# Last attention of a four-layer gated block: half of head 0's maximum taken while the scores are still computed, and the rows of reciprocals made by a matmul in the even units

## The reference, cut to what matters

```python
q = jnp.einsum('bnd,de->bne', ln, Wq)
kv_in = jnp.concatenate([xn, ln], axis=1)
kv = jnp.einsum('bnd,de->bne', kv_in, Wkv)
k, v = jnp.split(kv, 2, axis=-1)
q, k, v = (split_heads(q), split_heads(k), split_heads(v))
q = q * scale
sim = jnp.einsum('bhid,bhjd->bhij', q, k)
sim = jnp.where(full_mask[:, None, None, :], sim, max_neg)
attn = jax.nn.softmax(sim, axis=-1)
out = jnp.einsum('bhij,bhjd->bhid', attn, v)
out = out.transpose(0, 2, 1, 3).reshape(b, m, INNER)
out = jnp.einsum('bne,ed->bnd', out, Wout)
return layer_norm(out, g_o, b_o)
```

## Time and profile before

| | |
|---|---|
| median of 3 runs | 2177.15 us |
| the profiled execution's own time | 2167.44 us |
| its span on the core | 2165.5 us |
| PE busy | 1934.3 us (89%) |
| DVE busy | 1487.1 us (69%) |
| ACT busy | 975.6 us (45%) |
| POOL busy | 754.9 us (35%) |
| mean granted PE clock | 0.956 of full speed |

### The profile page before, as it was taken

How to read it: one execution, slowest core, us unless ns; L and a number is a source line. 1 busy time by engine, 2 the same in 40 slices (tenths; PEclk the granted TensorE clock), 3 DMA queues, 4 the chain that set the end, 5 groups by cost and what they waited for, 6 DMA issues and landing times.

```text
span 2165.5 us, 32060 instructions
## 1 busy us (share of the span) xinstructions
PE 1934.3 (89%) x11157; PEld 1304.9 (60%) x11157; DVE 1487.1 (69%) x2740; ACT 975.6 (45%) x2083; POOL 754.9 (35%) x1146
## 2 busy tenths in 40 slices
PE   6996999679999979979689999999989999998899
PEld 3883899434799958855545445545654555554544
DVE  5764111484344467968769998989778999988655
ACT  5662343333111431258744555545445555544445
POOL 1002011002322100000057666766546777766400
PEclk9997999889999999989899999999999999998999
DMA  3603899204599730020023333333222333332201
GB/s 111 201 1 119 275 324 330 85 0 158 182 322 323 251 111 1 1 83 1 1 49 75 78 76 75 77 73 78 58 51 72 78 78 77 79 72 71 53 1 39
DMA packets 191180, 226.79 MB, mean 105 GB/s; under 512 B 28939, under 2 KB 167085, under 8 KB 191021
## 3 DMA queue, kind: packets, MB, share of 16 engines
q1 hardware_dynamic: 183725, 201.98, 31.8%
q0 software_dynamic: 7296, 22.78, 3.1%
HBM read 127.64 MB, written 29.91 MB: 73 GB/s over the span
## 4 chain that ended last, share of the span: by engine, by line
PE 38%; DVE 11%; ACT 6%; issue 1%; ACTq 0%; DVEq 0%
PE ps L640 35%; ACT w_odd L1787 4%; DVE small L2519 4%; DVE small L2521 3%; DVE small L2522 1%; PE ps L1205 1%; PE ps L1213 1%; PE ps L1106 1%; ACT L1787 0%; DVE x_res L2485 0%; DVE small L2400 0%; PE ps L1206 0%; PE ps L1115 0%; DVE arena L2473 0%; DVE w_odd L2530 0%
## 5 line engine op out<-in xcount | busy, mean ns | idle before, releaser
L1898 POOL COPY arena<-w_odd 32x512 f32<-32x512 f32 x1024 | 625.5, 611 | 326.3 <-DVE w_odd L2530 274.0
L640 PE MATMUL ps<-arena,w_odd 128*128 128x128 f32 (+4 forms) x2352 | 449.2, 450 | 3.0 <-DVE arena L2192 1.2
L640 PE MATMUL ps<-arena 128*64 128x256 f32 (+4 forms) x3248 | 394.2, 372 | 8.6 <-DVE arena L2323 4.8
L1787 ACT ACTIVATE w_odd<-ps,small 128x1101 f32<-128x1101 f32 x256 | 301.8, 1179 | 95.3 <-DVE small L2519 53.1
L2530 DVE STREAM_TRANSPOSE w_odd<-w_odd 128x1024 f32<-128x1024 f32 x256 | 317.5, 1243 | 26.3 <-ACT w_odd L1787 17.8
L640 PEld LDWEIGHTS ps<-arena 128*64 128x64 f32 (+4 forms) x3248 | 259.3, 155 | 121.8 <-issue 24.7
L640 PEld LDWEIGHTS ps<-arena,w_odd 128*128 128x128 f32 (+3 forms) x2352 | 249.1, 190 | 108.8 <-issue 103.5
L2519 DVE TENSOR_REDUCE small<-ps 128x1 f32<-128x1101 f32 x128 | 166.8, 1303 | 65.8 <-PE ps L640 65.8
L1772 ACT ACTIVATE arena<-ps 77x256 f32<-77x256 f32 x128 | 48.7, 380 | 334.1 <-PE ps L1206 334.1
L1882 POOL DMA_INDIRECT token_rows<-arena x62 | 60.0, 968 | 292.4 <-DVE arena L2213 292.4
L2521 DVE TENSOR_REDUCE small<-ps 128x1 f32<-128x1024 f32 x128 | 155.5, 1215 | 0.0
(11 more groups left out here) (398 smaller groups left out, 3025.8 us busy)
## 6 DMA issues: line engine op xcount, KB each, us to landing
arena<-w_odd SPq DMA_DIRECT2D x1024, 64.0 KB
w_odd<-in_s_w SPq DMA_DIRECT2D x32, 1024.0 KB, 7.2
w_odd<-in_s_wgu SPq DMA_DIRECT2D x30, 704.0 KB, 5.8
w_even<-in_s_w SPq DMA_DIRECT2D x15, 1024.0 KB, 7.1
arena<-expert_rows_in SPq DMA_DIRECT2D x62, 130.0 KB, 4.5
w_odd<-in_s_wd SPq DMA_DIRECT2D x30, 256.0 KB, 3.6
out_feat<-in_s_wgu SPq DMA_DIRECT2D x10, 704.0 KB, 5.8
expert_rows_in<-zero_row POOLq DMA_DIRECT2D x1, 5070.0 KB, 32.0
```

Of the source, the lines that this page charges most:

```text
L640: return pe.matmul(o, lhsT, rhs, start=start, stop=stop, **kw)
L1787: act.activation(s6_p[u % 2][h], s6_sc[h], ACT.Exp, bias=s6_nm[:, u % 2, h:h + 1], accum_out=s6_sm[:, g % 2, 2 * (u % 2) + h:2 * (u % 2) + ...
L1898: pool.tensor_copy(s6_d[u % 4][32 * j:32 * j + 32, :, 256 * i:256 * i + 256], s6_pm[u % 2][32 * i:32 * i + 32, :, 256 * j:256 * j + 256]). ...
```

## The change

Five things change, all in `stage6`:

1. PE counts `a6_s` three times per unit: after the context keys, after keys 0 to 511 of both heads, and after keys 512 to 1023.
2. DVE takes head 0's maximum in two parts: bank 0 (512 columns) after the second count, the other 589 columns after the third, and the smaller of the two negated maxima by one more one-element instruction.
3. The copy that widened the reciprocals goes. PE makes the rows by four matmuls whose weights are a column of reciprocals read 64 times (stride 0) and whose moving operand is the identity, where it made two transposes.
4. These matmuls, `sums_turn`, and ACT's copy of their result move from the odd unit (before `weigh`) to the even unit before it (before the projection pieces), which changes the turns of banks 5 to 7.
5. DVE's reciprocal moves from the start of the odd unit after the pair to the end of the odd unit that closes the pair, behind its transposes.

```diff
-        s6_rb = [cut(AR, 14080 + 256 * i, 4, DH) for i in range(2)]
-        s6_main = psf[:, 3 * 512:3 * 512 + S]
+        s6_rest = [psf[:, 512:KV], psf[:, 3 * 512:3 * 512 + S]]
...
             batch = [("c", u - 1)] if turn else []
+            if even and 2 <= u < NU + 2:
+                batch += [("r", (u - 2) // 2)]
...
             if not even and 3 <= u < NU + 3:
-                batch += [("r", (u - 3) // 2), ("v", (u - 3) // 2)]
+                batch += [("v", (u - 3) // 2)]
...
                             last = mm(PS[:, 3 * h + i, :], s6_q[n % 2][r:r + 64, q0:q0 + P], s6_k[n % 2][r:r + 64, i * 512:(i + 1) * 512])
-                    last.then_inc(a6_s, 1)
+                        last.then_inc(a6_s, 1)
...
                     for i in range(2):
-                        last = pe.transpose(PS[:, bank, i * P:(i + 1) * P], s6_rb[g % 2][:, 2 * i:2 * i + 2].rearrange("p h d -> p (h d)"), ident[:, :])
+                        for h in range(2):
+                            r = 64 * h
+                            last = mm(PS[r:r + 64, bank, i * P:(i + 1) * P], s6_rc[:, g % 2, 2 * i + h:2 * i + h + 1].broadcast_to([P, DH]), ident[:, :])
                     last.then_inc(r6_mm, 1)
...
+                    if even and 2 <= u < NU + 2:
+                        sums_turn((u - 2) // 2)
                     if even and n < 16:
                         for i in (j, j + 1):
                             piece(n, i, free_bank(("w", n, i))).then_inc(r6_mm, 1)
                     if not even and 3 <= u < NU + 3:
-                        sums_turn((u - 3) // 2)
                         weigh((u - 3) // 2)
...
-                    if not even and 3 <= u < NU + 3:
-                        g = (u - 3) // 2
+                    if even and 2 <= u < NU + 2:
+                        g = (u - 2) // 2
                         bank = filled(("r", g))
                         act.activation(s6_r[g % 2], PS[:, bank, 0:2 * P], ACT.Copy).then_inc(r6_act, 1)
...
-                    if not even and 3 <= u < NU + 3:
-                        g = (u - 3) // 2
-                        dve.wait_ge(a6_p, 4 * g + 4)
-                        link(dve.reciprocal(s6_rc[:, g % 2], s6_sm[:, g % 2]))
-                        if g >= 2:
-                            dve.wait_ge(r6_mm, r6_no["r", g - 2] + 1)
-                        dve.tensor_copy(s6_rb[g % 2], s6_rc[:, g % 2].unsqueeze(2).broadcast_to([P, 4, DH])).then_inc(a6_rb, 1)
                     if u < NU:
-                        dve.wait_ge(a6_s, 2 * u + 1)
+                        dve.wait_ge(a6_s, 3 * u + 1)
                         link(dve.tensor_tensor(s6_both, s6_both, s6_mk[:, u // 64].unsqueeze(1).broadcast_to([P, 2, C]), ALU.add))
                         dve.tensor_reduce(s6_cm[:, u % 2, 1:2], s6_both[:, 1], AX.X, ALU.max, negate=True)
-                        dve.wait_ge(a6_s, 2 * u + 2)
-                        dve.tensor_reduce(s6_nm[:, u % 2, 0:1], s6_sc[0], AX.X, ALU.max, negate=True).then_inc(a6_mx, 1)
-                        m = s6_nm[:, u % 2, 1:2]
-                        link(dve.tensor_reduce(m, s6_main, AX.X, ALU.max, negate=True))
-                        dve.tensor_tensor(m, m, s6_cm[:, u % 2, 1:2], ALU.min).then_inc(a6_mx, 1)
+                        dve.wait_ge(a6_s, 3 * u + 2)
+                        dve.tensor_reduce(s6_cm[:, u % 2, 0:1], psf[:, 0:512], AX.X, ALU.max, negate=True)
+                        dve.wait_ge(a6_s, 3 * u + 3)
+                        for h in range(2):
+                            m = s6_nm[:, u % 2, h:h + 1]
+                            link(dve.tensor_reduce(m, s6_rest[h], AX.X, ALU.max, negate=True))
+                            dve.tensor_tensor(m, m, s6_cm[:, u % 2, h:h + 1], ALU.min).then_inc(a6_mx, 1)
...
                             dve.transpose(s6_pm[u % 2][:, h], s6_pm[u % 2][:, h]).then_inc(t6_done, 1)
+                        if not even:
+                            g = u // 2
+                            if g >= 2:
+                                dve.wait_ge(r6_mm, r6_no["r", g - 2] + 1)
+                            dve.reciprocal(s6_rc[:, g % 2], s6_sm[:, g % 2]).then_inc(a6_rb, 1)
```

## The result

| | before | after |
|---|---|---|
| median of the timed runs, same chip | 2178.18 us | 2142.48 us |
| ratio, 95% interval | | 0.9833, 0.9813 to 0.9853 |
| the profiled execution's own time | 2167.44 us | 2142.78 us |
| its span | 2165.5 us | 2140.9 us |
| PE busy | 89% | 91% |

The change is 35.7 us faster, and a second comparison gave 0.9829 (0.9813 to 0.9845). I had forecast 2162.5 us with a range from 2143.0 to 2181.0: the direction was right, the size less than half of what came, and the time just outside the range.

What follows compares the result with a forecast made beforehand. PE, DVE and ACT were taken to wait for each other in a ring, PE alone bounding odd units. Terms of -12.6, -0.5, +4.8 and -6.4 us took 2167.44 to 2152.7; with 9.7 us profile-to-median difference, 2162.5 us, range 2143 to 2181.

Steps and rivals of the forecast that it cites:

- The odd unit: PE's odd unit without the transposes, weighing starting 2.72 us after the scores: 6.76 us instead of 7.00.
- The even unit, PE's side: PE's even units, 6.86 us less idle plus the new matmuls: 7.21, 6.83, 6.42 and 5.96 us.
- I take 0.95: Delay of the even unit's projection pieces by eight new matmul passes and gaps: 0.95 us, from 0.63 to 1.15.
- The even unit, the ring's side: Even unit's chain after splitting head 0's maximum: 6.5 us against 6.86, setting the pace in two of four even units.
- the ring: PE, DVE and ACT waiting for each other in turn: scores, maxima, minima, exponential, next scores; 6.5 us per unit forecast.
- At 0.3 each: The two one-element minima on DVE, each 0.16 to 0.66 us depending on POOL's copies, taken as 0.3 us each.
- ACT's copy of the rows: ACT's 0.37 us copy ahead of head 0's exponential in the even unit, ending at 4.0 us: hidden.
- The second kind of pairs: The 15 pairs of units 78 to 107, with the next stage's transposes: 13.64 us instead of 13.67, -0.5 us.
- The pairs with the output projection: Six pairs with output projection or stage's end in PE's even unit; new matmuls in the open: +4.8 us.
- The clock: Four odd units slowed to 8.59 us by PE's lower clock after long waits return to normal: -6.4 us.
- The sum: All terms over the attention's pairs of units: -12.6, -0.5, +4.8 and -6.4 us, together -14.7 us.
- Rival A: Cheap new matmuls in PE's even unit, 0.41 to 0.65 us; DVE sets the pace: -30, 2147 us; chance 0.25.

Runs made afterwards that it cites:

- the split kernel: Kernel before with only head 0's maximum split in two and both minima taken by two-cell reductions; 0.9813 of the kernel before.

## Why the prediction was wrong, point by point

**The odd unit.** 6.76 forecast, 6.68 to 6.79 measured; the weighing starts 2.64 us after scores that follow a busy PE and 2.75 us after those that follow a wait, for 2.72. Right.

**The even unit, PE's side: the failed step.** "I take 0.95." I added 0.95 us to the slack that the idle column shows, for 7.21 and 6.83 us; measured were 6.87 and 6.50. Two errors of 0.17 each. First, the passes cost 0.052 us, not up to 0.101: I read the weighing's 0.101 us per load as what a load takes, when it was the pace of the moves behind it. The first piece starts 0.78 us later than before (3.33 - 2.55), not 0.95. Second, the idle column counts from the modelled end of the last matmul, and the next scores can start 0.16 us before that end (1492.78 + 0.59 against 1493.21), so the slack was 0.77 us where the earlier trace rows show 0.60. The mechanism, that the even unit is the longer of PE and ring, held; the term was too large. It is 0.17 us a pair of the 0.29 by which the pair is shorter than forecast (13.23, not 13.52), some 6 us over 37 pairs.

**The even unit, the ring's side: mis-sized too.** "At 0.3 each" is 0.6 us for the two minima. In the two kinds of even unit that the ring decides they take 0.39 us (u % 8 = 4) and 0.57 us (6) together, and the rest of the ring is 5.82 us (with two reductions of 0.155 it is 6.13 in the split kernel), not 5.90: hence 6.21 and 6.39 us, not 6.5. That is 0.10 us a pair, 4 us over 37 pairs. By the forecast's own sum, minima of 0.16 us would have changed little (13.49 for 13.52), since PE's side, too high, stood over them. I had found the wait for POOL, took it for a price of the instruction that would come twice instead of once, and spread it evenly. It is a matter of phase: POOL's eight copies start with the end of DVE's transposes, and whether a minimum falls inside a copy depends on everything in between. In the new phase the second minimum, at the chain's end, never waits, and the first often does. Removing that wait alone, in the kernel before, is worth 0.92%, more than half as much as the whole change. Why the phase moved as it did was not tried apart.

**ACT's copy of the rows.** I called it hidden. With both minima at 0.15 us the ring is 6.13 us where the copy stands in the odd unit and 6.21 where it stands in the even one, so it can cost 0.08 us.

**The second kind of pairs.** 13.64 forecast, 13.30 measured ((1872.29 - 1672.72) / 15): 5 us more, by the same two errors.

**The pairs with the output projection.** I had +4.8 us for six, 3.2 for four; the four of the first batch went from 84.7 to 88.7 us, so +4.0. Right in size, but not the new matmuls alone: in three of the four even units PE now also waits 1.0 to 1.1 us ahead of the projection pieces, for DVE's emptying of the weighed values (before, 0.4 us at most), and the odd units there became shorter.

**The clock.** I had four half-clock units saved, -6.4 us. In the trace before, six ordinary odd units of 8.6 us or more followed waits (31, 47, 69, 75, 111, 119), at a granted clock of 0.80 or less, in the trace after none of them is under 1.00 (unit 111, with a wait of its own, still takes 8.15 us, from 10.58). The length of the wait alone doesn't tell: before, the scores of units 7, 15, 23, 39 and 55 also waited 1.84 or 1.85 us and kept 1.00. The windows view after, from 1420 to 1440 us, where unit 47 lies, as the earlier trace rows, and from 1947 to 1975 us, where PE still waits 3.0 and 2.8 us before units 121 and 123 (columns: length; busy us and instructions of PE, PEld, DVE, ACT and POOL; granted clock; DMA share; GB/s):

```profile
1420.00:1440.00 20.00, 19.41 (x116) 10.51 (x113) 19.25 (x33) 10.38 (x21) 14.56 (x24) 1.00 0.34 81
1947.00:1975.00 28.00, 22.22 (x138) 11.65 (x136) 25.11 (x42) 12.14 (x22) 19.48 (x33) 0.90 0.32 78
```

Granted 1.00 in the one and 0.90 in the other. About 10 us, 3 more than forecast. That the waits cause the lower clock is the reading of where they stand; no run changed the wait alone.

**The sum.** -23 for 37 pairs, -5.5 for 15, -10 for the clock, +4 for the projection: -34.5, and the stage is 34.8 us shorter. Rival A was nearly the case in its pairs (13.28 and 13.35, against 13.23 and 13.30), but partly by luck: it had passes and gaps at 0.41 to 0.65 us, and they took 0.78, with 0.17 of slack that it didn't know of; it had one kind of even unit bound by PE, and there are two; and it had too few half-clock units. I gave it 0.25 and cut the range just where it lay.

## What to carry to other kernels

When an instruction of one element takes several times its own length, look at which engine's instruction ends at the same instant, and try the operation in another form, here a reduction with one SBUF input: that is a cheaper first step than to shorten the chain around it. One input is not a guarantee, as the widening copy shows. Read such durations by kind of unit: a median over all hid a wait of 0.40 us here. In a ring of engines where one is at work nearly all the time, two shortenings that each bring 26 us bring 36 together; take the price of each from the engine that is the floor, unit by unit, and shift work between units before removing more of it. Count a slack as the idle column plus what the pipelined end of a matmul hides (0.16 us here).

## What the runs showed of the hardware

- The wait of a DVE instruction for POOL is set by phase: 0.54, 0.28 and 0.16 us for the same instruction in the kernel before, 0.16 to 0.60 us after, and a step of 0.38 us per even unit in the time.
- A DVE copy with one SBUF input that widens 4 columns to 256 takes 0.29 us beside none of POOL's copies and ends 0.15 us after the running one otherwise, 0.72 us for most.
- Fp32 matmul passes with 64 weight columns and 128 moving ones, alternating between the two column halves, run at 0.053 us each, weight load included, though all use the same 128 rows; changing the tile shape costs 0.16 to 0.17 us each way.
- Two chips differ by 14 to 16 us in the same kernel (2164 and 2167 against 2180 us), and the traces place the difference in the earlier stages: the attention starts at 1093 to 1099 us on one and, in the kernels run on the other, at 1107 to 1109 us.
